# Folding the expert parameters beside the item scatter of a mixture-of-experts layer

## What is computed

```python
logits = xt @ Wr + br                      # xt: normalised rows, 6250 x 256; 8 experts
top_p, top_idx = top_k(softmax(logits), 2)
weights = top_p / top_p.sum(-1)
xn = (xt - mean) * rsqrt(var + eps)
xe = xn * ln_g[e] + ln_b[e]                # for each expert e
h = gelu(xe @ W1[e] + b1[e])               # W1[e]: 256 x 1024
y = h @ W2[e] + b2[e]                      # W2[e]: 1024 x 256
out = sum over the two chosen experts of weights * y
```

## Time and profile before

| | us |
|---|---|
| median of 3 runs | 20676.14 |
| the profiled execution, its own time | 20766.81 |
| its span, first to last instruction | 20765.1 |
| `moe_route`, from its first DVE instruction to the sort | 390 |
| counting, ranking and placing of the items | 37 |
| item scatter, first issue to last | 126 |
| load of the slots to the first instruction of the tiles | 100 |
| the 108 tiles | 1220 |
| recurrence at the end (rest of the span after 11.3 ms) | about 9400 |

### The profile page before, as it was taken

One profiled execution on the slowest core, in us unless ns is written; L12 is line 12 of the kernel. 1 busy time (PEld: TensorE's weight loads), 2 busy tenths in 40 slices (PEclk: granted clock), 3 DMA queues, 4 the chain that ended last, 5 costly groups with the idle time before them and its releaser, 6 DMA issues. The chain is left out here.

```text
span 20765.1 us, 681244 instructions
## 1 busy us (share of the span) xinstructions
PE 13394.2 (65%) x247461; PEld 10139.7 (49%) x247462; DVE 11922.9 (57%) x68644; ACT 6330.8 (30%) x42794; POOL 5965.1 (29%) x6174
## 2 busy tenths in 40 slices
PE   2324665442258745545555888888888888888887
PEld 1212222332135523433433777777777777777776
DVE  3324555555211334444445777777777777777777
ACT  0000664100001100100101555555555555555555
POOL 3452555555445566466464000000000000000000
PEclk6555777776579966766766555555555555555555
DMA  0000001222011233333232000000000000000000
GB/s 18 9 13 8 1 1 31 75 69 46 14 49 26 59 88 88 81 88 88 80 89 63 4 4 4 4 4 4 4 4 4 4 4 4 4 4 4 4 4 16
DMA packets 378633, 606.03 MB, mean 29 GB/s; under 512 B 184109, under 2 KB 258574, under 8 KB 375212
## 3 DMA queue, kind: packets, MB, share of 16 engines
q0 software_dynamic: 249728, 468.82, 8.8%
q1 hardware_dynamic: 126124, 99.43, 1.5%
HBM read 505.48 MB, written 62.30 MB: 27 GB/s over the span
## 5 line engine op out<-in xcount | busy, mean ns | idle before, releaser
L2267 PE MATMUL lr_ZI<-ls_h,ls_V 128*128 128x1 f16 x150000 | 5008.2, 166 | 1677.1 <-DVE ls_h L2316 1417.8
L2267 PEld LDWEIGHTS lr_ZI<-ls_h,ls_V 128*128 128x128 f16 x150000 | 4488.9, 104 | 2684.6 <-DVE ls_h L2316 2648.7
L2284 ACT ACTIVATE ls_tg<-lr_ZI 128x2 f32<-128x2 f32 x12500 | 2150.0, 172 | 4622.2 <-PE lr_ZI L2267 4530.5
L672 PE MATMUL prop_sum<-prop_G,prop_S 128*128 128x256 f32 x4992 | 1864.6, 522 | 1884.9 <-issue 968.0
L2311 DVE TENSOR_TENSOR_SCAN lr_c<-ls_tg,ls_one_hc 128x2 f32<-128x2 f32 x12500 | 2123.3, 171 | 1429.3 <-ACT ls_tg L2284 1310.8
L2267 PE MATMUL lr_ZO<-ls_h,ls_V 128*128 128x1 f16 x75000 | 2864.6, 165 | 0.0
L658 POOL DMA_INDIRECT prop_G<-hop_table,prop_idx x2496 | 2363.3, 947 | 1621.6 <-issue 710.4
L2223 POOL COPY ls_HT<-ls_h 128x250 f32 x50 | 19.8, 395 | 9359.0 <-DVE ls_h L2321 9359.0
L2267 PEld LDWEIGHTS lr_ZO<-ls_h,ls_V 128*128 128x128 f16 x75000 | 2483.3, 104 | 0.0
L672 PEld LDWEIGHTS prop_sum<-prop_G,prop_S 128*128 128x128 f32 x4992 | 1175.0, 258 | 2574.5 <-issue 2266.7
L2316 DVE TENSOR_TENSOR ls_h<-ls_to 128x1 f16<-128x1 f32 x12500 | 2025.7, 163 | 480.1 <-ACT ls_to L2289 16.8
(11 more groups left out here) (427 smaller groups left out, 15465.2 us busy)
## 6 DMA issues: line engine op xcount, KB each, us to landing
prop_G<-hop_table,prop_idx POOLq DMA_INDIRECT x2496
me_W<-in_L_ffn_W SPq DMA_DIRECT2D x16, 1024.0 KB, 10.9
moe_out<-me_Ys SPq DMA_DIRECT2D x108, 128.0 KB
gm_AG<-gat_atable,gm_idx POOLq DMA_INDIRECT x832
all_X<-gat_table,gs_idx POOLq DMA_INDIRECT x832
hop_table<-ht_T SPq DMA_DIRECT2D x50, 256.0 KB, 2.1
sd_records<-sc_rec,sc_place POOLq DMA_INDIRECT x784
ss_records<-me_recs,me_places POOLq DMA_INDIRECT x540
```

What stands on the lines that cost most here:

```text
L672: nc.tensor.matmul(ps[u][:, 0:D], S[:, r % 2, u, :], G[:, r, u, :], start=True, stop=True).then_inc(mm, 1)
L2267: mm = nc.tensor.matmul(place(hf, bank, col, 1), (V2 if part == "21" else V1)[:, q, ROWS.index(row), :], hx[:, prev, q, 1:2], start=False, ...
L2284: nc.scalar.activation(tg[:, s % 2, m, :], place(hf, m, col, 2), ACT.Tanh, scale=back).then_inc(gates[m], 1)
```

## The change

The fold leaves `moe_experts` and becomes a class, `ExpertFold`. Its instructions are the same, in three places:

- SP issues the eight loads of W1 at the start of `moe_route`, behind Wr and br, ahead of the store of the table. They count on a semaphore of their own.
- The other loads, the PE products, all DVE work of the fold and the load of W2 are put on SP, PE and DVE in the block of the item scatter. PE waits for W1 only.
- The item scatter loses its ring. POOL issues 100 written-out indirect DMAs straight from `place` and `rec`; before a group of five it waits until the group before last has landed.

The edge scatter is closed in a block of its own, right behind `moe_route`. The phases are nested anew so that W1 stays in SBUF from the routing on. `combine_and_open`, the hop transforms and everything else are as before.

```diff
@@ sort_items @@
-        ring_place = ph.sb("ring_place", [P, 2, HU], I32)
-        ring_rec = ph.sb("ring_rec", [P, 2, HU, RW])
...
         turns = ph.sem("turns")
-        ringed = ph.sem("ringed")
         sent, before = ph.indirect(k, C // 2)
         with ph.block() as block:
+            @block.gpsimd
+            def _(pool):
+                for c in range(C):
+                    j, turn = c // HU % 2, c // (2 * HU)
+                    if c % HU == 0:
+                        if turn:
+                            pool.wait_ge(sent[j], before + turn * (16 * HU))
+                        pool.sem_inc(turns)
+                    nc.gpsimd.indirect_dma_start(
+                        out=records[:, :], out_offset=bass.IndirectOffsetOnAxis(ap=place[:, c:c + 1], axis=0),
+                        in_=rec[:, c, :], in_offset=None).then_inc(sent[j], 16)
+                for j in range(2):
+                    pool.wait_ge(sent[j], before + C // 2 * 16)
+
+            @block.sync
+            def _(sp):
+                aside.sync(sp, tb_dram)
+
             @block.vector
             def _(dve):
-                def fill_ring(c0, j):
...
+                aside.vector(dve)
+
+            @block.tensor
+            def _(pe):
+                aside.tensor(pe)
@@ moe_route @@
                 sp.dma_start(b1[:], br.unsqueeze(0)).then_inc(loaded, 16)
+                fold.load_first(sp)
                 sp.wait_ge(tabled, 1)
@@ new class @@
+    def load_first(self, sp):
+        for e in range(NE):
+            sp.dma_start(self.W1s[:, e], self.W1[e].rearrange("(k p) h -> p k h", p=P)).then_inc(self.loaded1, 16)
...
+    def sync(self, sp, tb_dram):
...
+        for e in range(NE):
+            sp.dma_start(self.W2s[:, e], self.W2[e].rearrange("(k p) d -> p k d", p=P)).then_inc(self.loaded2, 16)
+        for q in range(3):
+            sp.wait_ge(self.parted, q + 1)
+            sp.dma_start(self.B3[q * BPART:q * BPART + NE, :], self.part[:]).then_inc(self.spread, 16)
+        sp.wait_ge(self.loaded2, 16 * NE)
+        sp.wait_ge(self.spread, 48)
...
+    def tensor(self, pe):
+        nc = self.nc
+        pe.wait_ge(self.ready, 1)
+        pe.wait_ge(self.loaded1, 16 * NE)
+        for n in range(HID // BANK):
+            for e in range(NE):
+                for c in range(KD):
+                    last = nc.tensor.matmul(self.psB[n][0:NE, :], self.bsel[:, e, c], self.W1s[:, e, c, n * BANK:(n + 1) * BANK],
+                                            start=(e == 0 and c == 0), stop=(e == NE - 1 and c == KD - 1))
+        last.then_inc(self.biased, 1)
@@ moe_layer @@
-        with Phase(nc, "mob") as pb:
-            scatter = Scatter(nc, k, pb, later, WITH_FINISH, WITH_ROUTE, 8)
-            moe_route(nc, k, X, Wr, br, table, expert, weight, lambda pool: scatter.piece(pool, scatter.rounds))
...
+        with Phase(nc, "mow") as pw:
+            fold = ExpertFold(nc, k, pw, ln_g, ln_b, W1, b1, W2, b2)
+            with Phase(nc, "mob") as pb:
+                scatter = Scatter(nc, k, pb, later, WITH_FINISH, WITH_ROUTE, 8)
+                moe_route(nc, k, X, Wr, br, table, expert, weight, lambda pool: scatter.piece(pool, scatter.rounds), fold)
+                with pb.block() as block:
+                    @block.gpsimd
+                    def _(pool):
+                        scatter.close(pool)
+            fold.rest()
+            with Phase(nc, "mef") as pf:
...
+                sort_items(nc, k, "ms", bins, ItemPrep(nc, k, expert), MC, G, NE, MT, MT, 5, 1, records,
+                           pos_out=where[:].rearrange("p k b -> p (k b)"), tile_bin=tbk, aside=fold)
...
+            moe_experts(nc, k, table, slots, tbk, fold, Y, later)
```

More of the change, by code:

```diff
@@ L180, in sort_items @@
 def sort_items(nc, k, name, bins, prep, C, G, NBIN, TM, TROW, HU, RW, records, pos_out=None, tile_bin=None, prefill=None,
-               staged=None, beside=(None, None, None), held=None, pieces=1, also=None):
+               staged=None, beside=(None, None, None), held=None, pieces=1, also=None, aside=None):
     NG = C // G
@@ L1272, in compute, with moe_route @@
             ch.mark(nc.vector.tensor_copy(rec[:, j * NB:(j + 1) * NB, 0], node[:]))
-def moe_route(nc, k, X, Wr, br, table, expert, weight, beside):
+def moe_route(nc, k, X, Wr, br, table, expert, weight, beside, fold):
     with Phase(nc, "mr") as ph:
@@ L1392, in moe_experts @@
+def moe_experts(nc, k, table, slots, tile_bin, fold, Y, later):
     with Phase(nc, "me") as ph:
[L1393 to L1396, removed]
+        W1s, W2s, B3, oht = fold.W1s, fold.W2s, fold.B3, fold.oht
         oh = ph.sb("oh", [BROWS, 2, P], BF16)
@@ L1693, in moe_layer, with _ @@
         slots = ph.sb("slots", [P, MT])
-        with Phase(nc, "mob") as pb:
-            scatter = Scatter(nc, k, pb, later, WITH_FINISH, WITH_ROUTE, 8)
-            moe_route(nc, k, X, Wr, br, table, expert, weight, lambda pool: scatter.piece(pool, scatter.rounds))
-            G = 10
-            bins = pb.sb("bins", [P, MC + G])
-            tb_dram = sort_items(nc, k, "ms", bins, ItemPrep(nc, k, expert), MC, G, NE, MT, MT, 5, 1, records,
-                                 pos_out=where[:].rearrange("p k b -> p (k b)"), tile_bin=tbk)
-            loaded = pb.sem("loaded")
-            with pb.block() as block:
-                @block.sync
-                def _(sp):
-                    sp.dma_start(slots[:], records.rearrange("(p t) r -> p (t r)", p=P)).then_inc(loaded, 16)
-                    sp.wait_ge(loaded, 16)
-                @block.gpsimd
-                def _(pool):
-                    scatter.close(pool)
-        moe_experts(nc, k, table, slots, tbk, tb_dram, ln_g, ln_b, W1, b1, W2, b2, Y, later)
+        with Phase(nc, "mow") as pw:
[9 more added lines that the diff above has]
+            with Phase(nc, "mef") as pf:
+                G = 10
+                bins = pf.sb("bins", [P, MC + G])
+                fold.open(pf)
+                sort_items(nc, k, "ms", bins, ItemPrep(nc, k, expert), MC, G, NE, MT, MT, 5, 1, records,
+                           pos_out=where[:].rearrange("p k b -> p (k b)"), tile_bin=tbk, aside=fold)
+                loaded = pf.sem("loaded")
+                with pf.block() as block:
+                    @block.sync
+                    def _(sp):
+                        sp.dma_start(slots[:], records.rearrange("(p t) r -> p (t r)", p=P)).then_inc(loaded, 16)
+                        sp.wait_ge(loaded, 16)
+            moe_experts(nc, k, table, slots, tbk, fold, Y, later)
         then(Y, where, weight)
```

158 lines of the change are left out of this document (62 added, 96 removed).

## The result

The changed kernel took 20605.87 us (median of 5 runs, 20581.71 to 20611.35) against 20676.14 us (5 runs). The medians differ by 70.3 us (0.34%); the ratio on record is 0.9958, which would be 87 us, with the interval 0.9945 to 0.9971 (60 to 114 us). The forecast was 20591, the range 20574 to 20636. The profiled execution took 20611.35 us, its span was 20609.6 us. The two spans differ by 155 us: the profile of before stands 90.7 us above its median, that of after 5.5. So the spans can't be subtracted as a whole; only the stages can be compared, and those only with care, as the experiments show.

What follows compares the result with a forecast made beforehand. Two stretches in line on different engines: POOL's 128 us item scatter, then 99.9 us of load, PE, DVE. Terms -99.9 + 3.5 + 1 - 1 + 6 + 3 + 2 = -85.4 us took 20676.1 to 20591, range 20574 to 20636.

Steps and rivals of the forecast that it cites:

- The fold's place: Between the slots' load and the tiles: the fold's 99.9 us go, 3.5 us stay for landing, block change and clears.
- The block and the ring: Extra block behind the routing for the edge scatter's close, +1 us; POOL starting the item scatter without a ring, -1 us.
- The late signals: Fold beside item scatter: after 14 free us, 47 matmuls at 1.9 us each; DVE goes on at 5738, ends at 5774.
- +6: End of the item scatter: the fold's late end moves the slots' load to about 5777; +6 us, from 0 to +37.
- +2 for POOL: Item scatter: W2's load and DVE's sixteen scalings lengthen POOL's issues; +2 us, from 0 to 11.
- The rule that I weighed there: Item scatter: tensor-with-scalar instructions can hold the port pair shared with GpSimd, so descriptors wait; it would make the term 11 us.
- W1 beside the routing: Routing: landing W1 might hold POOL's edge scatter for up to 22 us; +3 us taken, from 0 to +18.
- Signs that I had set: Included 1.26 us item issues, scalings 1.4 us apart, routing 390 to 395 us, later stages changing by at most 10 us.
- Hidden: Fold beside the item scatter ends ahead of it, signals about 1.4 us per matmul; about 20582 us, chance 0.20.
- Starved to the end: Fold beside item scatter: DVE hears of PE only when the scatter is over; about 20622 us, chance 0.14.
- Slower, through one shared path: Fold and item scatter share one path, so their work adds up; +20 us, or +53 at the upper bound; chance 0.03.

Runs made afterwards that it cites:

- one-product run: Changed kernel with the fold's products cut to one per bank (2 of 32), late chip, one run: 20588.39 us.
- W1 alone moved: Kernel before with W1 loaded in the routing and the fold in its old place, late chip, ten runs: 20628.76 us, ratio 0.9993.
- the written-out scatter: Kernel before with the item scatter written out, without its ring and with nothing beside it, prompt chip, one run: 18302.57 us.
- the three experiments on a late chip: Changed kernel with W1 loaded behind the edge scatter, 20556.54 us; changed kernel with 2 of 32 products, 20588.39; kernel before with W1 loaded in the routing, 20628.76.
- the two runs meant to vary the burst: Changed kernel with the fold's 32 products made twice, 18200.55 us, and with 18 of the 32 products, 18231.84 us; both prompt chip, one run each.
- the one meant to vary the pace: Changed kernel with eight small POOL memsets behind every issue of the item scatter, prompt chip, one run: 18210.81 us.
- W1 beside the items: Changed kernel with W1 loaded in the item scatter's block ahead of W2, not in the routing, prompt chip, four runs: 18220.80 us, ratio 0.9951.

## Why the prediction was right, and where it was not

**The fold's place: right.** Forecast -99.9 + 3.5 = -96.4; 99.9 became 2.9 us, -97.0. That is the gain, on both kinds of chip (99.6 to 101.1 before, 2.8 to 3.0 after on the prompt ones, there in four variants of the changed kernel). The order of the load was as foreseen: W1 was there, PE started 6.6 us after the first item scatter (5636.24 against 5629.61).

**The block and the ring: right**, and small. Counting to the first item scatter took 0.7 us less (forecast -1). The extra block lies in the routing's row, where the prompt chips show it alone: 234.0 against 233.4 us (forecast +1).

**The late signals: the forecast hit by two errors that cancel.** DVE was forecast to be told 103.6 us after the first scatter (5738 in before's time, less 5634.4) and was told after 117.7. Taken as I did, from 14 us on and over 47 records, that is (117.7 - 14)/47 = 2.2 us each, between the bounds of 1.40 and 2.62 and above the 1.9 that I took. What failed inside the sum is the next step: "Its tail then has 16 scalings at 1.40 instead of 0.67 (22 us)". They took 0.67 us each, in one piece, and the whole tail 19.0 us instead of 36. The 1.40 us of the earlier trace rows was read as a price of every DVE instruction that signals beside a scatter. In the changed kernel most scalings came too late to test this; in the one-product run all sixteen lay beside the scatter, and they took the same 10.69 us. Why the fifty L160 of the earlier trace rows were spaced by 1.40 us and the scalings not, no run shows; a line of signals that moves slowly and holds an engine up only when it is full would fit both, but that is a guess. Had only one of the two errors been made, the fold's end would have been missed by 14 or 17 us; that it was hit within 3 is luck. Fold's end: forecast 139.6 us after the first scatter, measured 136.6.

**What the stage grew by: the size was near, the reason wrong.** Forecast +6 as the fold's end would push the load of the slots, and +2 for POOL. Measured +3.7 in all, and the one-product run has 3.6, with its fold over 98 us ahead of the load of the slots. So the term of +6, put down to the fold's end, was nothing here. Some 2.1 us are POOL's own issues: first to last 127.1 against 125.0 us; on prompt chips the stage grew by 2 us as well. They come mostly from DVE's splits of the biases (L1460, L1463): the five issues beside them are together 2.2 us longer than 0.96 us each, the one beside the scalings 0.1 us.

The rule that I weighed there (the Trainium skill, SBUF — State Buffer, "Who interferes with whom") would, by the prediction's estimate, have made the sixteen scalings cost 11 us. In the one-product run, where all of them lie beside the scatter, the eight issues there take 1.02 us (one 1.07) instead of 0.96, 0.5 us together, so here it does not hold at that size. The long instructions of the earlier trace rows, which the prediction took for the rule, are not of that kind: L1190 has two inputs. Of two-input instructions the same section says that they meet GpSimd's reads, and it infers that writing descriptors is not touched by them. The trace does not agree: an issue that starts 0.4 us behind the start of the subtraction L1463 (two SBUF inputs, 1.48 us) takes 1.92 or 1.93 us, in every kernel where they meet so; the others beside it take 1.05 to 1.51 us.

The other 1.6 us of the stage on late chips lie between the last issue and the load of the slots (13.9 against 12.3); the one-product run has 13.7, the kernel with W1 alone moved 12.3, and on prompt chips the written-out scatter has 12.0. Their cause is open, and the written-out scatter alone was not tried on a late chip.

**W1 beside the routing: too low on this kind of chip.** Forecast +3 (0 to +18), routing "390 to 395". Measured 402.9, 403.4, 403.1 and 402.8 in four profiles with the load in that place against 391.0 in the one profile of before. POOL was not held, as the pricing had it: the edge scatter beside the load kept 0.96 us per issue and ended 220.3 us after the routing's start, 2.6 earlier than before. So the mechanism named ("If that held POOL's edge scatter") was not it. What changed is how many of the 50 turns of the logits were through when the scatter's late signals ended. The last slow turn of before, and the last two of after:

```profile
5431.77 0.17 DVE L1318 COPY mr_L<-mr_L 128x8 f32 x1 [12.94 <-remote]
```

```profile
5403.49 0.17 DVE L1316 COPY mr_L<-mr_L 128x8 f32 x1 [19.87 <-remote]
5414.73 0.17 DVE L1316 COPY mr_L<-mr_L 128x8 f32 x1 [10.61 <-remote]
```

The first is the 11th turn, 226.7 us after the routing's start; the last is only the 6th, 225.6 us after it. Each turn behind the scatter takes 2.63 us, so five turns more, less the 1.1 us, are 12.0 us: the whole growth of 11.9. With the changed kernel's other two profiles on late chips it is the 6th turn as well, with W1 loaded behind the edge scatter the 8th, with W1 alone moved the 7th. The waits in the view of the logits' tile tell the same: before, and then after:

```profile
  remote: 52.0, 6
  issue: 39.5, 8
```

```profile
  remote: 74.9, 5
  issue: 72.5, 9
```

Waits put down to "remote" and "issue" grew from 91.5 to 147.4 us. These sums include time that no one would have used otherwise, so they aren't 56 us of path. On a prompt chip the load costs nothing (234.0 with, 234.1 without it). Loaded behind the edge scatter, where no load is beside it, W1 leaves the routing at 397.9 and not at 391.0, so the load beside the scatter can't be the whole reason; with W1 there but the fold in its old place, it is 399.4. Why fewer turns came through is open, and whether all 12 us are the change's can't be said from one profile of before on a late chip.

**Signs that I had set: some of them came.** I had said that I would be wrong if the item scatter's issues stretch, and six of its hundred did, to 1.93 us at the worst; they cost 2 us. The scalings were to stand 1.4 us apart and the routing to take 390 to 395 us; neither was so. And I would be wrong if stages behind changed by more than 10 us. The combination took 23.8 us less, and the tiles 50.6 us less. The profile's waits in the tiles of before, and then of after:

```profile
ACT me_H L1518 <- remote: 360.5, 52, 22.8
DVE me_HT L1642 <- remote: 292.3, 47, 22.6
```

```profile
ACT me_H L1528 <- remote: 303.8, 55, 17.6
DVE me_HT L1652 <- remote: 248.5, 51, 17.4
```

The tiles issue edge scatters, so on a late chip they wait for late signals, and this part varies: 1168.9, 1171.8 and 1186.3 us in three profiles of the same changed kernel, and 1175.7 in the kernel with the fold in its old place. The combination was 4170 to 4178 us in the six profiles on late chips behind the first, that kernel's included. On prompt chips the tiles of seven profiles, of six kernels, lie between 944.0 and 944.3. So nothing shows that the fold's move bought the 50 us, and the kernel with the fold in its old place has most of them too. The time ahead of the layer, whose instructions no kernel changes, tells the same: 5205 us before, 5189, 5179 and 5185 after, 5138, 5173 and 5143 in the three experiments on a late chip, but 3724 to 3730 on prompt chips.

**What stays open.** On late chips the stages touched sum to -82 us (-97.0 + 3.7 + 11.9 - 0.7), the three ratios to about -90 (0.44% of 20676), with -82 within their intervals; the medians differ by 70, 100 and 89 us. W1 alone moved should have given -33 by its stages and gave -10, with an interval down to -33; the medians of that kernel and the changed one on the same chip differ by 89 us, where the stages touched explain 49 (58.5 against 2.9 us in front of the tiles, less the routing and the scatter), and their profiled executions by 36. Differences of 20 to 50 us between kernels arise there in stages that no edit touches, and I can't tell them from the edit's. Open too is the price of a late signal by itself: the two runs meant to vary the burst beyond the one-product run, and the one meant to vary the pace, were on prompt chips.

**The rivals.** Hidden (20582): it had the fold over by 5750 in before's time; it was over at 5771, but still 4.4 us ahead of the slots' load, so in effect the fold did hide. Of the 24 us from 20582 to 20606 the routing took 12; the other 12 lie in no stage that the change touches. Starved to the end (20622): DVE's signal came 9.4 us ahead of the last issue, not behind it. Slower, through one shared path: no; POOL kept its pace. On prompt chips the hidden rival holds: the fold is over 45 us ahead of the last issue even with twice the products, and the gain is 0.49% [0.32, 0.66] with W1 beside the items.

## What to carry to other kernels

Two stages that stand in line on different engines, and don't need each other's results, are worth their shorter length when laid side by side. The gain came out alike (0.4 to 0.5%) whether signals beside the scatter were late or prompt (on a prompt chip measured with W1 beside the items, not for the changed kernel itself). The reason is the slack of the longer stage: undisturbed, the fold would have been over 85 us ahead of the load of the slots (141.0 less 6.6, 30.1 and 19.0), the late signal took 81 of them, and 4 were left. What must be priced is the slack of the cover against the worst lateness, not the undisturbed work. Before a stage-by-stage difference of a few per cent is believed, look whether stages that the change doesn't touch differ as much; and where they do, get a second profile of the kernel before.

## What was not expected of the hardware

The kernel before takes 20639 to 20725 us on some chips and 18287 to 18306 us on others, and the difference lies in the stages in which indirect DMAs issued by GpSimd run beside other engines: the routing 391 against 233 us, the tiles 1220 against 944, the time ahead of the layer 5205 against 3728. The item scatter with nothing beside it takes 137 us on both, and the fold with no scatter beside it 100 us. The stage of the recurrence, which has no such DMAs, takes 9474 to 9508 us on both. On the late chips a signal from PE to DVE behind 64 records beside the scatter came 78 to 81 us late, in four profiles; on a prompt one 0.1 us late, behind 128. The granted clock doesn't explain it: in the two windows of the ranking, 32 and 546 matmuls in 100 us, it is 0.50 both times, the lower level (1.2 GHz). No run here shows what makes a chip late.

Second, on both kinds of chip DVE's sixteen tensor-with-scalar instructions over 128x1024 float32 lengthen GpSimd's scatter issues beside them by 0.06 us each. A subtraction of 8x1280 elements with both inputs in SBUF doubles an issue that starts 0.4 us behind it, from 0.96 to 1.92 us, and lengthens the others beside it to between 1.05 and 1.51.
